# Attention layers of a graph network: windows of nodes divided, turned and counted into the batch statistics while edge rows are still being gathered

## The chip, the cores and the metric

The kernel runs on one core of a Trainium2 chip. The metric is the device time of one execution in microseconds. The engines are TensorE (PE in the profile; PEld is its weight load), VectorE (DVE), ScalarE (ACT), GpSimd (POOL) and SyncE (SP). SBUF and PSUM are the on-chip memories; PSUM has eight banks, B0 to B7 in the code.

## What is computed

A graph with 6250 nodes of 128 features and 100000 edges goes through two relational layers and then, after a layer norm, through two graph attention layers. The change concerns only the attention layers. One of them is, cut to what matters (the edges here include one loop per node):

```python
xw = (x @ W).reshape(n, H, FH)                     # H = 4 heads of 32
al_s = einsum('nhf,hf->nh', xw, a_src); al_d = einsum('nhf,hf->nh', xw, a_dst)
e = leaky_relu(al_s[src] + al_d[dst], 0.2)
m = segment_max(e, dst); ee = exp(e - m[dst]); den = segment_sum(ee, dst)
out = segment_sum((ee / den[dst])[:, :, None] * xw[src], dst) + b
h = elu(batch_norm(out))                           # mean and variance over all nodes
```

The batch norm needs the mean and variance of every feature over all 6250 nodes, so nothing of it can be finished before the last node's sum is.

## The kernel before, in words

The nodes are split into 49 windows of 128 (`NW`). The edges are sorted by destination and cut into 832 slots of 128 edges (`NS`), each of which belongs to one window; 32 slots are a chunk (`CH`), 26 chunks a layer (`NC`). For each slot POOL issues one indirect DMA that gathers 128 rows of 132 numbers into a ring of 96 slots (`Gr`, line 1889); before it reuses a place it waits for the product of the slot 96 earlier, and for the gather 16 earlier.

Per chunk the attention weights of its edges are computed by a chain of small steps in `prep`, which exists once per engine and is run one chunk ahead, a step after each slot. DVE makes the selection matrices (line 937, four per slot in the first eight slots) and the scans of the running maximum (954 to 1006), ACT casts and copies (1368 to 1421), PE transposes (1705, 1726, 1744) and picks the destination's part (1719). DVE then multiplies eight slots' rows at a time by their weights (`weigh`, line 1013).

Per slot, PE multiplies the selection matrix by the gathered rows (line 1770) into bank `s % 3`, and DVE adds the bank into the window's row of the accumulator `AC` (`add`, line 1033), two slots behind (`LAG`). The accumulator holds per window 128 sums, 4 denominators and 4 maxima; the address comes from registers that are loaded 16 at a time. Before PE writes a bank it waits for the addition three slots back. Each engine runs its own list of instructions in the order written here; semaphores are the only coupling.

When all slots are added (end of `gat_vector`'s loop) the end of a layer runs: DVE computes from denominators, maxima and the node's own logits two weights per node and head (lines 1063 to 1082, with an exponential on ACT, line 1430), then POOL multiplies the node's own row by one (line 1904), DVE or POOL the sums by the other (lines 1091, 1906), DVE adds the two (line 1095), PE transposes the windows (line 1781), ACT adds the bias on the way from PSUM to `OT` (line 1435), DVE takes the statistics of four windows at a time (`bn_stats`, line 1098) and aggregates them (line 1101). Then come centring (line 1114), elu, and the projection for the next layer or the output (lines 1120 to 1133).

A list of turns, made on the chip from the sorted edges, says which windows are complete after which slot: `NTURN` is 84 turns for the 49 windows, turn `k` at slot 96 + 9k; a turn without a new window names a spare window. The relational layers already use it. `rest` is a loop over windows that the list left out, skipped by a branch when none was.

## Time and profile before

| what | us |
|---|---|
| median of three timed runs | 5546.97 (5546.96 to 5551.64) |
| the profiled execution | 5593.81 |
| its span, first to last instruction | 5592.0 |
| layer 0 of the attention: first gather to centring | 2764 to 4153 |
| layer 1: first gather to the end | 4181 to 5592 |

Times in views are microseconds from the span's start. "Idle before" is time in which the engine had nothing running, with what ended it; "issue" means that nothing the profile shows ended it, "remote" that the release came from something it cannot name. A wait for several semaphores is put down to the last.

### The profile page before, as it was taken

Reading aid. Unit: us, or ns where it says so; the run is one execution under the profiler, and the core shown is the slowest. Engines: PE = TensorE matmul, PEld = TensorE weight load, DVE = VectorE, ACT = ScalarE, POOL = GpSimd, SP = SyncE. Lnnn points to the kernel's source line nnn. Section 1 sums busy time; section 2 is a strip of 40 time slices with the busy share of each in tenths; the row PEclk is TensorE's granted clock in tenths of the full one; section 3 lists DMA queues with packets and bytes.
Section 4 is the critical chain, followed back from the end, with each engine's and each line's share of the span. In section 5 each row is a group of like instructions: output and inputs, shape, how many; then the busy total and the mean of one; then the engine's idle time right before and its main releaser. Section 6 shows DMA issues by size and latency. Waiting matters only on the chain.

```text
span 5592.0 us, 63654 instructions
## 1 busy us (share of the span) xinstructions
PE 3147.6 (56%) x12887; PEld 2272.1 (41%) x12887; DVE 2561.5 (46%) x9589; ACT 1064.3 (19%) x2505; POOL 3194.9 (57%) x3310
## 2 busy tenths in 40 slices
PE   7946666676734444444415555655651555555555
PEld 3434333343423333333314444444540444444444
DVE  6433333333333443444515555555571555555557
ACT  3301111121200000000102222222230222222223
POOL 0166666666266666666466666666526666666651
PEclk9957777777855555555555555555565555555556
DMA  6513333333322222222122222222102222222221
GB/s 238 228 44 111 124 121 118 118 119 123 115 71 53 55 54 54 55 54 56 35 48 45 45 45 45 45 45 45 39 26 49 46 44 45 45 45 45 45 43 47
DMA packets 168746, 395.78 MB, mean 71 GB/s; under 512 B 57590, under 2 KB 92468, under 8 KB 151092
## 3 DMA queue, kind: packets, MB, share of 16 engines
q0 software_dynamic: 103872, 215.70, 16.8%
q10 hardware_dynamic: 37968, 103.60, 4.8%
q1 hardware_dynamic: 26532, 72.39, 3.5%
q8 instruction: 126, 2.06, 0.2%
q14 instruction: 248, 2.03, 0.1%
HBM read 230.11 MB, written 161.35 MB: 70 GB/s over the span
## 4 chain that ended last, share of the span: by engine, by line
PE 34%; issue 22%; another core or an unknown queue 21%; DVE 13%; ACT 3%; POOL 2%; DVEq 2%; DMA 1%; SPq 1%; ACTq 0%; POOLq 0%
PE B L1770 9%; PE B L1650 8%; PE B L1550 6%; DVE AC L1033 3%; PE B L1612 3%; DVE AC L852 3%; PE B L1705 2%; PE B L1719 2%; ACT hold L1376 1%; POOL Gr L1889 1%; DVE Sr L937 1%; DVEq L308 1%; POOL Gr L1872 1%; DVE Sr L840 1%
## 5 line engine op out<-in xcount | busy, mean ns | idle before, releaser
L1889 POOL DMA_INDIRECT Gr<-Gtab,SRC x1664 | 1617.4, 972 | 1010.6 <-issue 471.4
L1872 POOL DMA_INDIRECT Gr<-Ttab,GID x1568 | 1501.8, 958 | 1045.6 <-issue 413.4
L1650 PE MATMUL B<-Gr,Sr 128*128 x3328 | 916.8, 402 | 723.7 <-issue 381.3
L1770 PE MATMUL B<-Gr,Sr 128*128 128x136 f32 x3328 | 1059.8, 462 | 402.2 <-DVE AC L1033 187.8
L1650 PEld LDWEIGHTS B<-Gr,Sr 128*128 128x128 f32 x3328 | 742.0, 279 | 1104.2 <-issue 1100.0
L1033 DVE TENSOR_TENSOR AC<-AC,B 128x136 f32 x1664 | 486.9, 293 | 1135.1 <-PE B L1770 470.8
L1770 PEld LDWEIGHTS B<-Gr,Sr 128*128 128x128 f32 x3328 | 786.4, 304 | 520.5 <-issue 243.6
L852 DVE TENSOR_TENSOR AC<-AC,B 128x128 f32 x1664 | 476.3, 286 | 937.8 <-remote 400.2
L1550 PE MATMUL B<-XW,hT 128*128 128x512 f32 x672 | 474.5, 798 | 90.3 <-ACT Sr L1202 32.9
L1705 PE MATMUL B<-identb,hold 128*128 128x128 bf16 x1664 | 251.9, 305 | 464.3 <-ACT hold L1376 259.5
L840 DVE TENSOR_SCALAR Sr<-iota,DL 128x128 f32<-128x128 f32 x1664 | 494.3, 299 | 15.8 <-issue 10.9
L1368 ACT CAST hold<-Sr 128x512 bf16<-128x512 f32 x416 | 257.6, 619 | 977.3 <-remote 500.1
L1705 PEld LDWEIGHTS B<-identb,hold 128*128 128x128 bf16 x1664 | 181.3, 138 | 524.5 <-ACT hold L1376 279.5
L937 DVE TENSOR_SCALAR Sr<-iota,DL 128x128 f32<-128x128 f32 x1664 | 373.8, 300 | 19.3 <-issue 18.9
L1202 ACT COPY Sr<-B 128x512 f32<-128x512 f32 x336 | 195.0, 585 | 648.2 <-PE B L1550 396.9
L1376 ACT COPY hold<-B 128x512 bf16<-128x512 bf16 x416 | 240.3, 584 | 147.7 <-PE B L1719 80.1
L1013 DVE TENSOR_TENSOR Gr<-Gr,B 128x1024 f32<-128x1024 f32 x202 | 245.2, 1214 | 3.4 <-issue 3.4
L1719 PE MATMUL B<-A,hold 128*128 x1664 | 163.2, 186 | 97.3 <-issue 44.4
L1719 PEld LDWEIGHTS B<-A,hold 128*128 128x128 bf16 x1664 | 148.1, 119 | 146.7 <-issue 131.7
L524 DVE COPY hT<-B 128x128 f32<-128x128 f32 x217 | 62.5, 289 | 309.2 <-remote 157.7
L1550 PEld LDWEIGHTS B<-XW,hT 128*128 128x128 f32 x672 | 136.8, 252 | 114.6 <-issue 41.7
L1612 PE MATMUL B<-XW,hT 128*128 128x512 f32 x392 | 179.0, 600 | 6.4 <-DVE hT L524 6.4
(275 smaller groups left out, 2358.2 us busy)
## 6 DMA issues: line engine op xcount, KB each, us to landing
Ttab<-Sr ACTq DMA_DIRECT2D x84, 1024.0 KB
Ttab<-Sr SPq DMA_DIRECT2D x51, 1024.0 KB
Gr<-Gtab,SRC POOLq DMA_INDIRECT x1664
Gr<-Ttab,GID POOLq DMA_INDIRECT x1568
Gtab<-Gr ACTq DMA_DIRECT2D x84, 66.0 KB
X1D<-Gr ACTq DMA_DIRECT2D x84, 64.0 KB
Gtab<-XW SPq DMA_DIRECT2D x7, 462.0 KB, 3.7
out<-Sr SPq DMA_DIRECT2D x12, 256.0 KB
```

Of the source, the lines that this page charges most:

```text
L840: e.tensor_scalar(out=selr(sn), in0=iota[:, :], scalar1=DL[:, sn:sn + 1], scalar2=None, op0=ALU.is_equal).then_inc(built_v, 1)
L852: e.tensor_tensor(a, a, B[RGCN_BANKS[L][sa % len(RGCN_BANKS[L])]][:, 0:P], ALU.add).then_inc(slot_add, 1)
L937: e.tensor_scalar(out=sel(s), in0=iota[:, :], scalar1=DL[:, s:s + 1], scalar2=None, op0=ALU.is_equal).then_inc(sel_made, 1)
L1033: e.tensor_tensor(a, a, B[s % 3][:, 0:CW], ALU.add).then_inc(gat_add, 1)
L1550: e.matmul(B[bk][:, :], hT[:, u % 2, :], wl[1][:, i * 512:(i + 1) * 512], start=True, stop=True).then_inc(row_mm, 1)
L1612: e.matmul(B[k][:, :], hT[:, w % 2, :], wl[0][:, k * 512:(k + 1) * 512], start=True, stop=True).then_inc(row_mm, 1)
L1650: e.matmul(B[banks[s % len(banks)]][:, 0:P], selr(s), Gr[:, bass.ds(o, P)], start=True, stop=True).then_inc(slot_mm, 1)
L1705: mm = e.transpose(bt[:, j * P:(j + 1) * P], sbf[:, g % 2, j * P:(j + 1) * P], identb[:, :])
L1719: mm = e.matmul(B[5][:, 12 * m:12 * m + 12], sts[:, g % 2, j * P:(j + 1) * P], A3[:, bass.ds(off(e, regs[m % 16], 12 * NW), 12)], start=Tr ...
L1770: e.matmul(B[s % 3][:, 0:CW], sel(s), Gr[:, (s % GR) * CW:(s % GR + 1) * CW], start=True, stop=True).then_inc(gat_mm, 1)
L1872: e.indirect_dma_start(out=Gr[:, (sn + 1) % TG * P:((sn + 1) % TG + 1) * P], out_offset=None, in_=Tt[L][:, :], in_offset=bass.IndirectOffs ...
L1889: e.indirect_dma_start(out=Gr[:, (s % GR) * CW:(s % GR) * CW + 132], out_offset=None, in_=T2[L][0:NPAD][:, :], in_offset=bass.IndirectOffs ...
```

## The change

Once a group of windows is complete, their weights are computed and the windows are multiplied, turned, biased and counted between the slots, by the list of turns. The table `CLOSE` gives four groups: from slot 400 on the weights for turns 0 to 33, one step per slot, then one turn every four slots from slot 414; turns 34 to 56 from slot 621, 57 to 70 every three slots from slot 741, 71 to 76 from slot 802. Turns 77 to 83 remain for the end, with a fifth round of weights. Every round computes the weights of all 49 windows.

- DVE: `mix` multiplies the window's sums and its own row by their weights into two small buffers; `close` takes the window's statistics two turns later, into the window's own row of `AC`.
- PE: `turn_window` turns both parts with two products against the identity that add up in one bank (2, at the end also 3), so no addition of the parts is left to DVE.
- ACT: `turned_rows` adds the bias and writes the turned window back into `AC`; ACT's steps of `prep` now stand one per slot like the others', with these in between.
- Slot products use banks 0 and 1 instead of 0, 1 and 2, and PE waits for the addition two slots back.
- POOL's multiplications at the end are gone; centring reads `AC` instead of `OT`; the aggregate reads 49 statistics instead of 13; SP issues the loads of `X1D` after the last slot product.

```diff
+CLOSE = ((399, 0, 34, 4), (606, 34, 57, 4), (726, 57, 71, 3), (787, 71, 77, 3))
+WEIGHTS = {b + 1 + i: (j, i) for j, (b, _, _, _) in enumerate(CLOSE) for i in range(14)}
+MIXED = {b + 15 + pace * (k - k0): k for b, k0, k1, pace in CLOSE for k in range(k0, k1)}
+CLOSED = {b + 15 + pace * (k - k0 + 2): k for b, k0, k1, pace in CLOSE for k in range(k0, k1)}
...
+        def weighed(e, j, w):
...
+            return (e.tensor_tensor(heads(part[0][:, j, :]), heads(AC[:, bass.ds(w * CW, P)]), weight(1), ALU.mult),
+                    e.tensor_tensor(heads(part[1][:, j, :]), heads(XW[:, bass.ds(w * CW, P)]), weight(0), ALU.mult))
+
+        def turn_parts(e, j, to):
+            e.matmul(to, part[0][:, j, :], ident[:, :], start=True, stop=False)
+            return e.matmul(to, part[1][:, j, :], ident[:, :], start=False, stop=True)
...
-                e.tensor_tensor(a, a, B[s % 3][:, 0:CW], ALU.add).then_inc(gat_add, 1)
+                if done[1]:
+                    e.wait_ge(endv.sem, done[1])
+                    done[1] = 0
+                e.tensor_tensor(a, a, B[s % 2][:, 0:CW], ALU.add).then_inc(gat_add, 1)
...
+            def mix(k, j):
+                n = L * NTURN + k
+                if k % 8 == 0:
+                    e.reg_load(turns[k // 8 % 2], WIN[0:1, k:k + 8])
+                e.wait_ge(endv.sem, endv.at("al", L * NB + j))
+                if n >= 2:
+                    e.wait_ge(ot_made, n - 1)
...
+                for ins in weighed(e, n % 2, off(e, turns[k // 8 % 2][k % 8], NW + 2)):
+                    ins.then_inc(o_sum, 1)
+
+            def close(k):
+                e.wait_ge(ot_made, L * NTURN + k + 1)
...
+                e.bn_stats(AC[:, bass.ds(w * CW + P, 6)], AC[:, bass.ds(w * CW, P)]).then_inc(bst_made, 1)
...
+                    if s in WEIGHTS:
...
+                        next(closing, None)
+                    if s in CLOSED:
+                        close(CLOSED[s])
+                    if s in MIXED:
+                        mix(MIXED[s], group[MIXED[s]])
...
+            finish(weights(NB - 1))
+            for k in range(LASTK, NTURN + 2):
+                if k >= LASTK + 2:
+                    close(k - 2)
+                if k < NTURN:
+                    mix(k, NB - 1)
+            rest(e, rest3_vector, f"r3v{L}")
...
+            def turn_window(k):
+                n = L * NTURN + k
+                e.wait_ge(o_sum, 2 * n + 2)
+                if n:
+                    e.wait_ge(ot_made, n - 1 if k > LASTK else n)
+                turn_parts(e, n % 2, turning_of(k)).then_inc(o_turned, 1)
...
-                    if s >= 3:
-                        e.wait_ge(gat_add, L * NS + s - 2)
-                    e.matmul(B[s % 3][:, 0:CW], sel(s), Gr[:, (s % GR) * CW:(s % GR + 1) * CW], start=True, stop=True).then_inc(gat_mm, 1)
+                    if s >= 2:
+                        e.wait_ge(gat_add, L * NS + s - 1)
+                    e.matmul(B[s % 2][:, 0:CW], sel(s), Gr[:, (s % GR) * CW:(s % GR + 1) * CW], start=True, stop=True).then_inc(gat_mm, 1)
                     if i < 12 or (i >= 14 and i % 2 == 0):
                         next(gen, None)
+                    if s - 2 in MIXED:
+                        turn_window(MIXED[s - 2])
```

On DVE, in the middle of a chunk of the attention, the list before reads (`L1033` is a slot addition and `L308` the wait and address ahead of it, `L943` a step of `prep`):

```order
L308 ISA [waits gat_added,gat_products]
L1033 TENSOR_TENSOR AC<-AC,B2 128x136
L308 ISA [waits gat_added,gat_products]
L1033 TENSOR_TENSOR AC<-AC,B0 128x136
L943 TENSOR_REDUCE hold<-B5 128x128 [waits prep_vector,prep_tensor]
L308 ISA [waits gat_added,gat_products]
L1033 TENSOR_TENSOR AC<-AC,B1 128x136
```

and in the changed kernel, at a slot that has a turn:

```order
L319 ISA [waits gat_added,gat_products]
L1096 TENSOR_TENSOR AC<-AC,B0 128x136
L1000 TENSOR_REDUCE hold<-B5 128x128 [waits prep_vector,prep_tensor]
L319 ISA [waits end_transposed]
L1167 REGISTER_ALU
L1167 BN_STATS AC<-AC 128x6
L319 ISA [waits bn_stats,end_transposed,end_vector]
L562 ISA
L562 TENSOR_TENSOR hn<-AC,GID 128x128
L563 ISA
L563 TENSOR_TENSOR hT<-XW,GID 128x128
L319 ISA [waits gat_added,gat_products]
```

Three operations, with their waits and address arithmetic, now stand between two slot additions. On PE, at a chunk's end (`L1770` is a slot product, `L1705` a transposition of `prep`), before:

```order
L1770 MATMUL B0<-Gr,Sr 128x136 [waits gat_added]
L1770 MATMUL B1<-Gr,Sr 128x136 [waits gat_added]
L1770 MATMUL B2<-Gr,Sr 128x136 [waits gat_added,weighed_vector]
L1770 MATMUL B0<-Gr,Sr 128x136 [waits gat_added]
L1770 MATMUL B1<-Gr,Sr 128x136 [waits gat_added]
L1705 MATMUL B3<-identb,hold 128x128 [waits prep_scalar]
```

and in the changed kernel:

```order
L1906 MATMUL B1<-Gr,Sr 128x136 [waits gat_added]
L1906 MATMUL B0<-Gr,Sr 128x136 [waits gat_added,weighed_vector]
L566 MATMUL B2<-ident,hn 128x128 [waits end_weighed]
L567 MATMUL B2<-ident,hT 128x128
L1906 MATMUL B1<-Gr,Sr 128x136 [waits gat_added]
L1906 MATMUL B0<-Gr,Sr 128x136 [waits gat_added]
L1834 MATMUL B3<-identb,hold 128x128 [waits prep_scalar]
```

The slot products alternate between two banks, and the turn's two products stand between them.

## Rows read from the trace of the kernel before

**Rows 1.** The page's head and part 1.
```profile
span 5592.0 us, 63654 instructions
PE 3147.6 (56%) x12887; PEld 2272.1 (41%) x12887; DVE 2561.5 (46%) x9589; ACT 1064.3 (19%) x2505; POOL 3194.9 (57%) x3310
```

**Rows 2.** Busy time by stretch: us, engines' busy us (instructions), PEclk, DMA share, GB/s.
```profile
3100.00:3900.00 800.00, 466.57 (x2348) 375.08 (x2348) 413.54 (x1524) 189.38 (x460) 506.33 (x525) 0.54 0.21 45
4062.00:4092.00 30.00, 24.32 (x133) 20.97 (x133) 22.26 (x83) 10.51 (x27) 4.69 (x3) 0.56 0.01 2
4111.40:4153.20 41.80, 13.29 (x49) 8.94 (x49) 39.13 (x53) 10.93 (x17) 22.26 (x16) 0.51 0.00 0
4153.20:4178.00 24.80, 16.03 (x98) 14.02 (x98) 21.33 (x56) 21.11 (x52) 0.00 (x0) 0.84 0.45 128
```

**Rows 3.** The same view of line 1033 (slot additions) alone.
```profile
3100.00:3900.00 800.00, 151.54 (x518) 0.54 0.21 45
4062.00:4092.00 30.00, 8.80 (x30) 0.56 0.01 2
```

**Rows 4.** Waits from 3100 to 3900: us, times, longest.
```profile
DVE AC L1033 <- PE B L1770: 161.0, 114, 7.0
POOL Gr L1889 <- issue: 133.1, 404, 1.6
DVE AC L1033 <- remote: 123.0, 49, 9.6
POOL Gr L1889 <- PE B L1770: 92.5, 86, 5.6
DVE AC L1033 <- DVE AC L1033: 26.1, 109, 0.9
```

**Rows 5.** Line 1387 (first copy of gathered rows): what it waited for, us, times.
```profile
  DMA Gr<-Gtab,SRC: 61.5, 2
```

**Rows 6.** Timeline of DVE, end of layer 0's attention: start, us, instruction.
```profile
4111.44 0.36 DVE L1063 TENSOR_TENSOR Gr<-XW 128x196 f32<-128x196 f32 x1
...
4115.06 0.36 DVE L1076 TENSOR_TENSOR Gr<-AC,Gr 128x196 f32<-128x196 f32 x1 [0.59 <-ACT Gr L1430]
...
4117.86 0.69 DVE L1091 TENSOR_TENSOR AC<-AC,Gr 128x512 f32<-128x512 f32 x1
...
4144.42 7.38 DVE L1098 BATCH_NORM_STATS2 bst<-Gr 128x6 f32<-128x512 f32 x13
4151.84 0.51 DVE L1101 BATCH_NORM_AGGREGATE bmv<-bst 128x2 f32<-128x78 f32 x1
...
4153.20 1.00 DVE L1114 TENSOR_SCALAR Gr<-Gr,bmv,bsc 128x512 f32<-128x512 f32 x2
```

**Rows 7.** Timeline of DVE, two products of one kind in a row.
```profile
4026.03 0.29 DVE L1026 TENSOR_TENSOR AC<-AC,scs 128x128 f32 x1
4026.24 0.16 DVE L1028 TENSOR_TENSOR AC<-AC,scs 128x4 f32 x1
```

**Rows 8.** Timeline of PE, slot products without a pause.
```profile
4019.68 3.59 PE L1770 MATMUL B<-Gr,Sr 128*128 128x136 f32 x14
```

**Rows 9.** Timeline, one slot product and its addition.
```profile
3309.24 0.53 PEld L1770 LDWEIGHTS B<-Gr,Sr 128*128 128x128 f32 x2
...
3309.29 0.80 PE L1770 MATMUL B<-Gr,Sr 128*128 128x136 f32 x2
...
3310.23 0.30 DVE L1033 TENSOR_TENSOR AC<-AC,B 128x136 f32 x1 [0.56 <-PE B L1770]
```

**Rows 10.** Groups: busy us, mean ns (ACT and aggregates).
```profile
L1435 ACT ACTIVATE Gr<-B,gcol 128x128 f32<-128x128 f32 x1 | 0.4, 359 | 0.0
...
L714 DVE BATCH_NORM_AGGREGATE mv<-st 128x2 f32<-128x6 f32 x84 | 15.3, 182 | 2.9
```

**Rows 11.** Timeline of DVE, slot additions back to back.
```profile
4096.15 0.29 DVE L1033 TENSOR_TENSOR AC<-AC,B 128x136 f32 x1 [0.21 <-DVE AC L1033]
```

**Rows 12.** Line 700 (load of eight registers).
```profile
L700 DVEq TENSOR_LOAD <-FF x11: 595/656/742, 1696.3 to 2738.9; - x11
```

More of the change, by code:

```diff
@@ L218, in build @@
         rl = Gr[:, NPAD:NPAD + 2048].rearrange("p (i j e) -> p i j e", i=2, j=2)
-        fin = Gr[:, NPAD + 2048:NPAD + 2048 + 6 * NW * 4].rearrange("p (k e) -> p k e", k=3)
+        fin = GID[:, 0:4 * NW * 4].bitcast(f32).rearrange("p (k e) -> p k e", k=2)
+        largest = wt[:, :, :].rearrange("p a b -> p (a b)")[:, 0:NW * 4].rearrange("p (w h) -> p w h", h=4)
+        share = st6[:, :, :].rearrange("p w k -> p (w k)")[:, 0:NW * 4].rearrange("p (w h) -> p w h", h=4)
+        turning = [B[2 + j][:, 0:P] for j in range(2)]
+        part = [hn[:, :, :], hT[:, :, :]]
+        wci = wc[:, :, :].rearrange("p a b -> p (a b)").bitcast(i32)
+        WIN, RSTW = wci[0:1, 0:NKP], wci[0:1, NKP:NKP + NW]
         flat = [Gr[0:RF, k * RL:(k + 1) * RL] for k in range(9)]
@@ L640, in tables_vector @@
             after("pwk1")
+            then(e.tensor_copy(WIN, PWK), "win")
+            after("win")
+            then(e.scalar_tensor_tensor(out=WIN[:, 1::2], in0=PWK[:, 1::2], scalar=float(NW + 1), in1=PWK[:, 1::2], op0=ALU.is_ge, op1=ALU.add), "win1")
             then(e.tensor_scalar(out=ORD, in0=PWK, scalar1=float(CW), scalar2=None, op0=ALU.mult), "ord")
@@ L893, in vector, with gat_vector @@
             for L in range(2):
-                gat_vector(e, L, vregs)
-        def gat_vector(e, L, vregs):
+                gat_vector(e, L, vregs, (wregs, xregs))
+        def gat_vector(e, L, vregs, turns):
             T = L * NC
@@ new lines, in weights, with ev, past @@
+            def weights(j):
+                def ev(ins, name):
+                    endv.done(ins, name, L * NB + j)
+                    if name in ("z1", "neg", "dn"):
+                        done[1] = endv.at(name, L * NB + j)
+                def past(name):
+                    e.wait_ge(endv.sem, endv.at(name, L * NB + j))
+                if L or j:
+                    e.wait_ge(bst_made, L * (NTURN + 1) + (CLOSE[j - 1][2] if j else 0))
+                ev(e.tensor_tensor(F(0)[:, 0], als, ald_, ALU.add), "z0")
+                yield
+                e.wait_ge(gat_add, L * NS + done[0])
+                ev(e.tensor_tensor(F(0)[:, 1], mmx, ald_, ALU.add), "z1")
+                yield
+                past("z1")
+                ev(e.scalar_tensor_tensor(out=fin[:, 1, :], in0=fin[:, 0, :], scalar=0.2, in1=fin[:, 0, :], op0=ALU.mult, op1=ALU.max), "lr")
+                yield
+                past("lr")
+                e.wait_ge(gat_add, L * NS + done[0])
+                ev(e.tensor_scalar(out=F(0)[:, 0], in0=den, scalar1=0.0, scalar2=-BIG, op0=ALU.is_le, op1=ALU.mult), "neg")
+                yield
+                past("neg")
+                ev(e.tensor_tensor(F(1)[:, 1], F(1)[:, 1], F(0)[:, 0], ALU.add), "pm")
+                yield
+                past("pm")
+                ev(e.tensor_tensor(largest, F(1)[:, 0], F(1)[:, 1], ALU.max), "mx")
+                yield
+                past("mx")
+                ev(e.tensor_tensor(F(0), F(1), largest.unsqueeze(1).to_broadcast([P, 2, NW, 4]), ALU.subtract), "sub")
+                yield
+                yield
+                yield
+                e.wait_ge(end_exp, L * NB + j + 1)
+                e.wait_ge(gat_add, L * NS + done[0])
+                ev(e.tensor_tensor(largest, den, F(1)[:, 1], ALU.mult), "dn")
+                yield
+                past("dn")
+                ev(e.tensor_tensor(largest, largest, F(1)[:, 0], ALU.add), "dn1")
+                yield
+                past("dn1")
+                ev(e.reciprocal(share, largest), "rec")
+                yield
+                past("rec")
+                e.wait_ge(o_sum, 2 * (L * NTURN + (CLOSE[j - 1][2] if j else 0)))
+                ev(e.tensor_tensor(F(0), F(1), share.unsqueeze(1).to_broadcast([P, 2, NW, 4]), ALU.mult), "al")
+                yield
+                yield
@@ L1035, in gat_vector @@
+            def close(k):
+                e.wait_ge(ot_made, L * NTURN + k + 1)
+                w = off(e, turns[k // 8 % 2][k % 8], NW + 2)
+                e.bn_stats(AC[:, bass.ds(w * CW + P, 6)], AC[:, bass.ds(w * CW, P)]).then_inc(bst_made, 1)
+            done = [0, 0]
+            group = {k: j for j, (_, k0, k1, _) in enumerate(CLOSE) for k in range(k0, k1)}
             finish(prep(0))
```

174 lines of the change are left out of this document (90 added, 84 removed).

## The prediction

> **What bounds the kernel now.** First the page's sums: span 5592.0 us, and no engine is full; PE is busy 56% and POOL 57% [rows 1]. The profiled execution took 5593.8 us, the median of the three timed runs is 5547.0, so 47 us less; what I add or take away I put on both alike.
>
> The change touches only the attention, so I next took the busy time by stretch [rows 2]: the steady part of layer 0's gathers (3100 to 3900), a piece in which gathers are no longer issued, and the stretch between the last slot and the centring. In the steady part PE is busy 58%, DVE 52%, POOL 63%: nothing full, so waits decide. The counts of slot additions (line 1033) give the pace [rows 3]: 518 in 800 us, 1.54 us per slot or 49 us per chunk of 32 slots; once gathers have stopped, 30 in 30 us, 1.0 per slot.
>
> Who holds whom? A gather takes POOL 506.33/525 = 0.96 us, plus 0.33 to issue, 1.29 in all, under 1.54; POOL waits 92.5 us for products of PE, that is for a free place among the 96 rows of the ring [rows 2, 4]. The other side does not wait for gathers: the copy that first touches a chunk's gathered rows waited for a DMA only twice, 61.5 us together, once at each layer's start [rows 5]. So **the consumer sets the pace**, PE, DVE and ACT in turn, and not POOL. DVE waits 161.0 us for PE, 123.0 for a release the profile can't name, and 109 of its 518 additions wait only for the addition before them [rows 4]. Every microsecond put into this loop counts unless it falls into one of those waits.
>
> After the last slot comes the piece that the change attacks: the weights from 4111.44, division and sum from 4117.86, statistics from 4144.42, the aggregate at 4151.84, centring at 4153.20 [rows 6]. That is 41.8 us per layer in which PE does 13.29 us of work [rows 2].
>
> **The change, term by term, for one layer (there are two alike).**
>
> *End of the layer, saved.* Left over are one round of weights, 6.4 us (4111.44 to 4117.86, with its 0.59 for the exponential) [rows 6], and 7 of the 84 turns. A turn: two DVE products at 0.21 start to start, taken from two operations of the same kind behind each other [rows 7]; then PE. The slot product runs in two passes, 14 passes in 3.59 us, 0.26 each [rows 8]; the turn is two such products, so four passes, 1.03 us of PE, and 0.85 + 0.51 = 1.36 us from its weight load to its end, by the 0.85 of one two-pass product [rows 9]; then 0.36 on ACT [rows 10], with 0.14 for each handing over (3310.09 to 3310.23) [rows 9]. One turn alone takes 0.42 + 1.36 + 0.36 + 3 x 0.14 = 2.5 us; with two pairs of buffers the next follow at 1.25. Seven: 2.5 + 6 x 1.25 = 10. The aggregate grows from 78 to 294 numbers: 182 ns for 6 and 507 for 78 give 4.5 ns each, so 1.5 us [rows 6, 10]; behind it stay 0.85, and two last statistics and the skipped rest loop are about 1.2 (an estimate: twice 0.28 as of the products, and a register load of 0.66 [rows 12]). Sum 6.4 + 10 + 1.5 + 0.85 + 1.2 = 20, **saved 22**. Bounds: turns at DVE's own 0.63 save 26, turns one after the other at 2.5 save 14.
>
> *77 turns within the slots, added.* On DVE two products and one statistics at 0.21 each, 0.63; on PE 1.03; on ACT 0.36, which at 189.38 busy of 800 has room [rows 2]. The two need not add up, since a turn's stages are slots apart. What covers them: an addition that waits only for its predecessor leaves 0.21 idle [rows 11], and 163 of 518 additions wait for something longer [rows 4]. Without any cover the path takes DVE's 0.63 where DVE leads, PE's 1.03 where PE leads, with full cover nothing. I take 0.5, nearest to DVE's row: PE waits for DVE's additions in order, so a piece put between two additions holds both engines, while PE's own piece can run beside DVE's scans and selections; and a fifth of the additions have their 0.21 to give. 77 x 0.5 = **+38**; bounds 0 and 77 x 1.03 = 79.
>
> *Four more rounds of weights, one step per slot.* Each 6.4 less the 0.59 wait, 5.8 us of DVE [rows 6]; three quarters of it reach the path by the same cover: 4 x 5.8 x 0.75 = **+17**; bounds 0 and 23.
>
> *Register loads.* Eight registers at a time, 0.66 us on DVE's queue, 0.08 per register [rows 12]; ten of these in the loop, about 0.4 each uncovered: **+4**; bounds 0 and 7. The Trainium skill ("Runtime: NRT & Kernel Launch", Instruction fetch mechanics) gives such a load about 200 ns per register, which would be 1.6 us a time and 16 us in place of 7 at most. The trace does not agree, and the row decides.
>
> *Two banks for slot products instead of three.* PE's product of slot s now waits for the addition of s-2, before for s-3. One bank's round is 0.85 from weight load to end, 0.14 to DVE, 0.30 of addition [rows 9]: 1.29 us. By three that is 0.43 per slot, below the 0.50 at which DVE adds back to back (0.29 and 0.21) [rows 11], by two it is 0.645. So each slot that now goes at DVE's 0.50 loses 0.145. These are 109 of 518 at least, 175 per layer, 25 us; all 832 would be 121 us. DVE also holds long pieces (the weighing of eight slots, the scans) behind which PE has two products ready where it had three. I take **+36**, nearer to the counted rows; bounds 0 and 60, since slots with more work than 0.645 in them cannot lose it.
>
> Nothing else is on the path: the last multiplications leave POOL, the loads of X1D on SP are issued earlier, and windows 50 and 51 are cleared at the program's start.
>
> **Sum:** 38 + 17 + 4 + 36 - 22 = 73 to 74 per layer, **148 for both**. The profiled time goes from 5594 to 5742, the median from 5547 to **5695**.
>
> **Rivals.**
> 1. *The two banks cost nothing.* Either the slower slots catch up in the waits for ACT, or PE's clock is granted more: 0.54 in the steady part, so mostly the lower of its two levels (1.2 GHz), 0.84 in the stretch of the elu and the projection [rows 2]; at the higher level a bank's round would be short enough. For it: PE waits for ACT and others, too. Against: rounds above are from the steady part itself. Then 2 x (59 - 22) = +74: 5621.
> 2. *The turning disappears in the waits*, the other side. DVE is idle 48% of the steady part, PE 42% [rows 2]; if each turn falls where its engine waits anyway, only the shorter end is left. It decides from the point where the loop gains less than 22 us per layer, 0.29 us per turn with all else free. Full cover gives 5547 - 44 = 5503. Against: once gathers stop, the same loop is busy 81% and 74% on PE and DVE, so much of the idle time is not in long waits.
> 3. *PE leads.* A turn costs its 1.03 on PE, weights and loads all of their own, banks the upper 60, the end saves 18: 79 + 23 + 7 + 60 - 18 = 151 per layer: 5849. For it: PE is the busiest once gathers stop, and semaphores come late in the steady part (the 123.0 us without a name [rows 4]), against which a third bank was a reserve.
> 4. *The turns are not done early*, so that nothing is saved: the table fixes their slots whatever the data are, so this is out unless a wait holds DVE at the first of a group; it would show as one long gap, and I give it no chance of its own.
>
> **How the numbers follow.** Forecast 0.47, its own range 5640 to 5780 by the bounds of the turn's price (0.3 to 0.65) and of the banks (20 to 50). Rival 1: 0.20. Rival 2: 0.13. Rival 3: 0.20. The range leaves out most of rival 2 and the far part of rival 3: 5550 to 5825. A measurement of this kernel can tell 0.2% (11 us) from no change. Of rival 2, 0.02 end within that, and the bottom of rival 1 adds 0.02, so faster 0.11, same 0.04, slower 0.85.
>
> **What would show it.** Right: the stretch from the last addition to the centring falls to about 20 us; the pace of the slots between 414 and 823 rises by a sixth of a microsecond or more, and that of slots before 400, where only the banks differ, by some 0.04; POOL waits longer for PE. Additions that follow each other stand 0.6 apart, no longer 0.50. Rival 1: slots before 400 keep their pace. Rival 2: all keep it. Rival 3: PE's idle time before slot products is gone. Wrong altogether: a pace set by gathers, with DVE or ACT waiting for DMAs in mid-layer.

## The result and the profile after

| | before | after | ratio, 95% interval |
|---|---|---|---|
| median of the timed runs, us | 5546.97 | 5589.35 | 1.0072 (1.006 to 1.0085) |
| profiled execution, us | 5593.81 | 5595.45 | |

The changed kernel is slower by 42 us (33 to 47 by the interval). The sign was forecast, the size was not: 148 us were expected, 5695 in place of 5589, though the range (5550 to 5825) holds it. The two profiled spans are almost equal by chance: the changed kernel's first slot addition of the attention came 27 us earlier, at 2819.8, while in the other runs with a kernel before at 5547 to 5607 us it comes at 2846 to 2858, with the change and without. So I compare by stretches of the attention.

The page of the kernel after, against [rows 1]: PE has 185 us more to do, DVE 95.
```profile
span 5593.2 us, 66830 instructions
PE 3332.4 (60%) x13461; PEld 2391.0 (43%) x13461; DVE 2656.0 (47%) x10114; ACT 1103.6 (20%) x2656; POOL 3156.6 (56%) x3279
```

Busy time by stretch (columns as in [rows 2]): the steady part, a piece after the last gather with six turns in it, the last slots with the start of the end, and then line 1096, the slot additions, in the first two.
```profile
3100.00:3870.00 770.00, 510.46 (x2391) 400.48 (x2390) 438.50 (x1627) 189.54 (x477) 485.54 (x502) 0.53 0.21 45
4038.00:4068.00 30.00, 22.96 (x133) 19.48 (x134) 20.24 (x80) 11.51 (x26) 0.00 (x0) 0.67 0.00 1
...
4111.50:4130.00 18.50, 9.29 (x38) 6.51 (x36) 11.57 (x34) 1.63 (x4) 0.00 (x0) 0.68 0.00 0
...
3100.00:3870.00 770.00, 146.12 (x500) 0.53 0.21 45
4038.00:4068.00 30.00, 5.79 (x21) 0.67 0.00 1
```
500 slots in 770 us are 1.54 per slot, as before [rows 3], although 41 turns and two rounds of weights lie in them. After the last gather it is 21 slots in 30 us where it was 30.

The waits in 3100 to 3870, a stretch 30 us shorter than that of [rows 4]:
```profile
DVE AC L1096 <- PE B L1906: 146.1, 158, 4.8
...
ACT hold L1478 <- remote: 115.7, 17, 11.0
PEld B L1906 <- DVE AC L1096: 109.4, 114, 5.0
POOL Gr L2023 <- PE B L1906: 95.7, 107, 2.7
...
DVE AC L1096 <- remote: 81.1, 31, 6.2
```
DVE's waits for PE and for releases without a name fell from 161.0 and 123.0 us in 800 [rows 4] to 146.1 and 81.1 in 770, at the same pace: the new work took the place of waits. POOL's wait for PE hardly grew (92.5 to 95.7).

Timeline of DVE at the end of layer 0's attention, to be read against [rows 6]:
```profile
4114.91 0.29 DVE L1096 TENSOR_TENSOR AC<-AC,B 128x136 f32 x1 [0.21 <-PE B L1906]
4115.41 0.29 DVE L1096 TENSOR_TENSOR AC<-AC,B 128x136 f32 x1 [0.21 <-PE B L1906]
...
4118.15 0.35 DVE L1112 TENSOR_TENSOR GID<-XW 128x196 f32<-128x196 f32 x1
...
4124.81 0.29 DVE L562 TENSOR_TENSOR hn<-AC,GID 128x128 f32 x1 [0.27 <-DVE GID L1147]
...
4138.06 0.27 DVE L1208 BATCH_NORM_STATS2 AC<-AC 128x6 f32<-128x106 f32 x1 [0.28 <-DVE AC L1167]
4138.36 1.48 DVE L1211 BATCH_NORM_AGGREGATE bmv<-AC 128x2 f32<-128x294 f32 x1
...
4140.70 1.00 DVE L1224 TENSOR_SCALAR Gr<-AC,bmv,bsc 128x512 f32<-128x512 f32 x2
```
From 4118.15 to 4140.70 are 22.6 us where there were 41.8.

The next table is worked out from the starts of the slot additions (line 1033, then 1096). It gives the microseconds from the addition of one slot to that of another, layer 0 and layer 1. Slots 96 to 400 have only the two banks and ACT's new order of steps as a change; 400 to 741 the first two groups of turns with the gathers running, and three rounds of weights, since the third group's round (slots 727 to 740) stands ahead of its turns; 741 to 831 the last 20 turns and one round. POOL issues its last gather about when slot 737 is added.

| slots | before | after | difference, mean |
|---|---|---|---|
| 0 to 96 | 203.2, 202.5 | 203.1, 204.7 | +1.0 |
| 96 to 400 | 470.2, 468.0 | 465.1, 463.3 | -4.9 |
| 400 to 741 | 514.4, 516.4 | 526.6, 525.5 | +10.7 |
| 741 to 831 | 76.8, 75.6 | 103.4, 102.7 | +26.9 |
| layer 0's last addition to layer 1's first | 149.6 | 130.0 | -19.6 |
| last addition to the end | 68.9 | 48.9 | -20.0 |

So the loop pays +34 per layer and the end gives back 20: 14 per layer, 28 in these two profiled executions, where the timed runs say 42. Most of the price lies in the last 90 slots; 57 turns, three rounds of weights and 741 slots with two banks cost about 7 us together.

### The profile page after: what moved, and what is told of

Same layout as the page of the kernel before. It is cut to its first block, busy times and chain, and to the rows that moved or that the text cites. A ratio compares the mean times of both kernels' runs of the same rounds, so it can differ in the third digit from the quotient of the medians.

```text
span 5593.2 us, 66830 instructions
## 1 busy us (share of the span) xinstructions
PE 3332.4 (60%) x13461; PEld 2391.0 (43%) x13461; DVE 2656.0 (47%) x10114; ACT 1103.6 (20%) x2656; POOL 3156.6 (56%) x3279
## 3 DMA queue, kind: packets, MB, share of 16 engines
q0 software_dynamic: 103872, 215.70, 16.7%
## 4 chain that ended last, share of the span: by engine, by line
PE 39%; issue 20%; another core or an unknown queue 17%; DVE 14%; ACT 3%; DVEq 3%; POOL 2%; DMA 2%; SPq 0%; ACTq 0%; POOLq 0%
PE B L1906 10%; PE B L1779 9%; PE B L1679 6%; PE B L1741 3%; DVE AC L909 3%; DVE AC L1096 3%; PE B L1834 2%; DVE Sr L994 2%; PE B L1848 2%; POOL Gr L2023 2%; DVEq L319 1%; DVE Sr L897 1%; PE B L1657 1%; ACT hold L1486 1%
## 5 line engine op out<-in xcount | busy, mean ns | idle before, releaser
L1906 PE MATMUL B<-Gr,Sr 128*128 128x136 f32 x3328 | 1167.2, 471 | 681.9 <-DVE AC L1096 368.4
L1698 PE MATMUL B<-wx,hT 128*128 128x136 f32 x168 | 67.4, 505 | 188.3 <-DVE hT L576 91.0
```

Of the source, the lines that this page charges most:

```text
L1906: e.matmul(B[s % 2][:, 0:CW], sel(s), Gr[:, (s % GR) * CW:(s % GR + 1) * CW], start=True, stop=True).then_inc(gat_mm, 1)
```

## Experiments

Two theories. **C**, the prediction's (called W in two of the expectations): the consumer (PE, DVE, ACT) sets the pace of the slots, and what is added to it counts unless it falls into a wait. **G**: while gathers run they set the pace, by their bytes, their number or POOL's issue, and only the 90 slots after the last gather are the consumer's. Each group of runs has its own time of the kernel before, taken beside it: 5607 us for the first four runs, 5595 for the next four, 4647, 4647 and 4646 for the last three groups. Ratios are to that time.

### Two banks alone

The kernel before with this alone:
```diff
-                    if s >= 3:
-                        e.wait_ge(gat_add, L * NS + s - 2)
-                    e.matmul(B[s % 3][:, 0:CW], ...
+                    if s >= 2:
+                        e.wait_ge(gat_add, L * NS + s - 1)
+                    e.matmul(B[s % 2][:, 0:CW], ...
```


> The kernel before with two banks for the slot products and nothing else. By the prediction's own term it is 2 x 36 = 72 us slower (5619). If the waits of the loop take that up (or if the loop is paced by the gathers), it is within 0.2% of the kernel before, 5547 +- 11. In the changed kernel the slots 96 to 400, where only the banks differ, kept their pace (465 against 470 us), so I now expect under 12 us.

Measured: 1.0031 (1.0019 to 1.0043), +17 us, 8.7 per layer where the sum had 36. Slots 741 to 831 took 84.4 and 84.3 against 76.8 and 75.6, so 8 us, or 0.09 per slot, nearly all in the stretch without gathers; slots 96 to 400 took 471.7 and 468.8, no difference.

Where slot additions follow each other with nothing between, the price of the bank can be read directly. First b_2banks, the stretch with its granted clock and three of its additions; then the changed kernel in the stretch of the additions shown above:
```profile
4123.80:4131.00 7.20, 6.96 (x22) 5.09 (x21) 3.25 (x11) 0.00 (x0) 0.00 (x0) 0.50 0.00 0
...
4129.21 0.29 DVE L1033 TENSOR_TENSOR AC<-AC,B 128x136 f32 x1 [0.51 <-PE B L1770]
4129.72 0.29 DVE L1033 TENSOR_TENSOR AC<-AC,B 128x136 f32 x1 [0.21 <-PE B L1770]
4130.52 0.30 DVE L1033 TENSOR_TENSOR AC<-AC,B 128x136 f32 x1 [0.51 <-PE B L1770]
```
```profile
4113.80:4118.00 4.20, 3.90 (x16) 2.34 (x16) 2.43 (x9) 0.00 (x0) 0.00 (x0) 1.00 0.00 0
```
At the lower level of PE's clock (0.50) two banks give 0.51 and 0.80 in turn, 1.31 for two slots. That is close to the prediction's 0.645 per slot, where three banks have 0.50 [rows 11]. At the higher level (1.00) additions with two banks stand 0.51 apart, as with three. Over all places in layer 0 where five additions stand in a row, the medians per slot are 0.66 with two banks at the lower level and 0.51 with three (worked out from their starts).

### Half the rows per gather

From slot 96 on each gather fetches 64 rows instead of 128, in the kernel before (b_half) and in the changed one (a_half); the products use old rows for the other half, so other edges are summed.
```diff
-    out=Gr[:, (s % GR) * CW:(s % GR) * CW + 132], ...
+    out=Gr[0:64 if s >= GR else P, (s % GR) * CW:(s % GR) * CW + 132], ...
```


> The kernel before, in which each attention gather from slot 96 on fetches 64 rows instead of 128 (the other half of each slot is left out, the result is not the reference's). If the gathers and what they bring with them set the pace of the slots while they run (theory G), slots 96 to 700 go from 1.54 us to 1.2 or less and the time falls by 200 us or more per layer, over 350 in all. If DVE and PE set it by their own work and their hand-overs (theory W), the pace stays within 5% of 1.54.

> The changed kernel with the same halved gathers. Theory G: with the gathers' delays gone the turning has no cover, the difference to the halved kernel before grows from 42 us to 90 or more. Theory W, waits between PE, DVE and ACT being the cover: the difference stays near 42 us.

Measured: 1.0015 (1.0005 to 1.0024) and 1.0110 (1.0094 to 1.0125); the pair stands 54 us apart, nearer to the 42 of the full pair than to the 90 or more of theory G by bytes. Busy time by stretch of b_half, then its line 1033, then the group of gathers in the same stretch:
```profile
3100.00:3900.00 800.00, 465.25 (x2328) 374.08 (x2328) 419.90 (x1545) 186.06 (x455) 483.54 (x525) 0.54 0.13 23
...
3100.00:3900.00 800.00, 153.32 (x525) 0.54 0.13 23
...
L1889 POOL DMA_INDIRECT Gr<-Gtab,SRC x525 | 483.5, 921 | 316.7 <-issue 147.6 <-remote 109.4 <-PE B L1770 59.7
```
The DMA moves 23 GB/s instead of 45 [rows 2] and the pace is 1.52, nearly as it was. Bytes don't set the pace. The gathers' queue counts 103872 packets as in the kernel before, so the number of packets is not tested by this. An issue of 64 rows still takes POOL 0.92 us, against 0.97.

### Half as many gathers

From slot 96 on every odd slot's gather is left out; its product and addition are made with old rows.
```diff
+                    if s >= GR and s % 2:
+                        continue
                     e.indirect_dma_start(
```


> The kernel before, in which from slot 96 of each layer on every odd slot's gather is left out (736 instead of 1472 gathers from there); its product and its addition are made with whatever rows lie in the ring, so the sums are those of other edges. What PE, DVE and ACT do is unchanged. Theory G (number of gathers): POOL's issue of one gather per slot, with the semaphore updates that come late while gathers run, sets the pace; then the pace of slots 96 to 400 falls from 1.54 toward the 1.0 per slot that stands where no gathers run (1.0 to 1.25), 2 x 736 x 0.3 to 0.5 is 440 to 740 us less than the kernel before. Theory C (the consumer, as in the prediction): the pace stays at 1.5 to 1.55 and the time within 30 us of the kernel before.

> The changed kernel with the same edit: every odd slot's gather from slot 96 on left out, the rest as it was; the sums are those of other edges. Compared with the kernel before under the same edit. Theory G: with the gathers out of the way nothing covers the turning and the lost bank, so this pair differs by much more than the 42 us of the full pair, by 90 to 150 us, as the prediction's terms would have it. Theory C: the difference stays at 40 to 55 us.

Measured: 0.8651 (0.8622 to 0.8679) and 0.9083 (0.9058 to 0.9108). The kernel before lost 754 us, at the upper end of what theory G expected (440 to 740), and the pair lies 242 us apart instead of 42, far more than the 90 to 150 expected. Of b_skip, slot additions and all engines by stretch, the group of gathers, and the longest waits of a_skip (3100 to 3400):
```profile
3100.00:3400.00 300.00, 87.09 (x299) 0.62 0.16 35
...
3100.00:3400.00 300.00, 237.41 (x1321) 200.28 (x1320) 231.97 (x877) 105.90 (x257) 144.84 (x150) 0.62 0.16 35
...
L1894 POOL DMA_INDIRECT Gr<-Gtab,SRC x150 | 144.8, 966 | 155.2 <-PE B L1773 126.9 <-issue 28.3
```
```profile
POOL Gr L2028 <- PE B L1909: 145.2, 91, 4.2
...
DVE AC L1099 <- PE B L1909: 58.6, 103, 2.2
PEld B L1909 <- DVE AC L1099: 50.5, 85, 1.4
```
299 slots in 300 us, with PE busy 79% and DVE 77%: this is the consumer's own pace, and it is the 1.0 of [rows 3] after the last gather. POOL has no releases without a name left to wait for; all its long waits are for PE. **Theory C falls for the kernel before, G stands**, by the number of gathers or what goes with it (the packets fall too, to 80320). And the pair shows what the change costs where nothing covers it, per layer:

| slots | b_skip | a_skip | difference, mean |
|---|---|---|---|
| 96 to 400 | 305.9, 307.0 | 332.7, 331.9 | +25.9 |
| 400 to 741 | 345.1, 343.5 | 421.7, 424.0 | +78.6 |
| 741 to 831 | 74.3, 75.0 | 103.4, 104.4 | +29.3 |

### One half of a turn at a time

The kernel before with two banks, and at the 77 slots of a layer either PE's two products or DVE's three operations of a turn, with results that nobody reads.
```diff
+                    if s - 2 in TURNS:
+                        e.matmul(B[2][:, 0:P], hn[:, 0, :], ident[:, :], start=True, stop=False)
+                        e.matmul(B[2][:, 0:P], hT[:, 0, :], ident[:, :], start=False, stop=True)
...
+                    if s in TURNS:
+                        n = TURNS.index(s)
+                        e.tensor_tensor(hn[:, n % 2, :], XW[...], ones[:, :], ALU.mult)
+                        e.tensor_tensor(hT[:, n % 2, :], XW[...], ones[:, :], ALU.mult)
+                        e.bn_stats(st6[:, n % 2, :], XW[...])
```


> The kernel before with two banks for slot products, and at the 77 slots of a layer at which the changed kernel turns a window PE makes the two products of a turn (of whatever the buffers hold, into a third bank that nobody reads); no DVE or ACT work of a turn, no weights, the end of a layer as before. The two banks alone came to 1.003 of the kernel before. If a turn's PE part is what the slots pay, the 57 early turns cost little (0 to 0.2 each) and the 20 late ones about 0.5 to 1.0 each: 1.003 plus 2 x (6 + 15) = 42 us, 1.009 to 1.011. If DVE's part is what they pay, this kernel stays at 1.003 to 1.005.

> The kernel before with two banks, and at the same 77 slots of a layer DVE makes the two multiplications and the one statistics of a turn into buffers that nobody reads; no PE or ACT work of a turn, no weights, no register loads, the end as before. If DVE's part is what the slots pay: 0.63 us for each of the 20 late turns and 0.1 to 0.2 for the 57 early ones, 2 x (13 + 9) = 44 us over the two banks alone, 1.009 to 1.012. If PE's part is, it stays at 1.003 to 1.005. If both come out at about 1.006, neither leads and the price lies in the holding of both engines.

Measured: 1.0073 (1.0048 to 1.0097) and 1.0067 (1.0043 to 1.0092), so the case "neither leads": either adds some 0.004 to the 1.0031 of the banks, little more than the intervals. In the last 90 slots PE's part takes them from 84.4 and 84.3 to 85.2 and 85.3, DVE's to 88.5 and 86.9, the whole change to 103.4 and 102.7. Of the 19 us between two banks alone and the whole change 14 are in neither part by itself. One round of weights is among them, and it is dearer there than at the end: two of its multiplications run beside three of POOL's.
```profile
4083.53 6.09 POOL L2031 TENSOR_TENSOR Gr<-Gr 128x1024 f32<-128x1024 f32 x3 [75.16 <-ACT scs L1531]
...
4083.80 2.06 DVE L1131 TENSOR_TENSOR GID<-GID,wt 128x392 f32<-128x392 f32 x1
4088.30 1.53 DVE L1140 TENSOR_TENSOR wt<-wt,GID 128x196 f32<-128x196 f32 x1
```
At the end of the layer the same two take 0.57 and 0.36, and the round 5.6 of DVE where it takes 8.2 here, in both layers; the same 8.2 stand in a_half, a_skip and a_again. In a_new, whose last round lies earlier, no such multiplication is slow. The other 6 us may be the handing over from DVE to PE to ACT and back; that was not taken apart further.

### Twenty turns fewer in the loop

The changed kernel with the first two groups only:
```diff
-CLOSE = ((399, 0, 34, 4), (606, 34, 57, 4), (726, 57, 71, 3), (787, 71, 77, 3))
+CLOSE = ((399, 0, 34, 4), (606, 34, 57, 4))
```


> The changed kernel with the first two groups only: 57 turns within the slots, all while gathers are issued, 27 at the end. The trace of the changed kernel puts 27 us per layer on the two late groups (20 turns, two rounds of weights), and at the end a turn costs about 1.25 us: 20 x 1.25 = 25 more there. So within 10 us of the changed kernel (5580 to 5590) if late turns cost the same in both places; 30 us or more slower if a turn at the end costs over 2 us.

Measured: 1.0129 (1.0111 to 1.0147). The end has 27 turns instead of 7 and takes 81.5 us from the last addition, not 48.9: 1.63 per turn, against the 1.25 of the prediction. The last 90 slots fall from 103.4 and 102.7 to 84.7 and 85.1, so 18 us for 20 turns and one round; without the third group's round slots 400 to 741 take 528.9 and 528.1, no less than with it. The two late groups cost 18 us per layer in the loop and save 33 at the end, so they are worth having; what they don't pay for is the lost bank, the early turns and the early rounds.

### POOL's own time, and gathers waited for sooner

A small memset on POOL ahead of every gather, and a wait for the gather 4 or 2 earlier where the kernel before has 16:
```diff
+                        e.memset(mv[:, s % 49, :], 0.0).then_inc(extra, 1)
...
-                    wait_gather(e, n - NSG)
+                    wait_gather(e, n - 4)
```


> The kernel before with one small memset (128x2 numbers that nobody reads) on POOL ahead of every gather from slot 96 of a layer on, 1472 in all. Theory G1 (POOL's own cycle of issue sets the pace): each memset, by some 0.1 to 0.2 us with its dispatch, is added to the pace: 150 to 300 us more. Theory G2 (while POOL issues gathers back to back the other engines' releases come late, and they catch up in POOL's pauses): what fills the time between two gathers replaces a pause, so the time rises by less than the memsets or even falls: -100 to +100 us. Theory C (the consumer sets the pace and POOL has slack): within 15 us of the kernel before.

> The kernel before in which POOL waits, ahead of each attention gather, for the landing of the gather 4 earlier instead of 16 earlier, so that its series of gathers without a pause are broken up. Theory G2: series of 10 to 15 gathers without a pause become short, the stretches in which PE, DVE and ACT all stand still (20% of the steady part) shrink, and the pace falls below 1.54 per slot: 30 to 300 us less. Theory G1: the wait adds to POOL's cycle or does nothing: 0 to 100 us more. Theory C: within 15 us.

> The same with a wait for the gather 2 earlier. If a gather needs over 2.5 us from issue to landing, the pace is set by that: half of it per slot. Theory G2: if the landing takes 2 to 3 us the pace is 1.3 to 1.5 with hardly any stretch in which all engines stand still, and the time is below the kernel before; theory G1: 50 us more or above.

> The changed kernel with the wait for the gather 4 earlier. Theory G2: it gains from the shorter series as the kernel before does, but less, since the turning then has less idle time to fall into: its distance to the kernel before under the same edit grows from 42 us toward the 242 us of the pair with half as many gathers. Theory G1: the distance stays at 42 us.

For this group the kernel before itself took 4647 us, a sixth less than at any time earlier. So these runs could not decide what they were made for, and showed something else. Measured: b_pool 1.0016 (1.0006 to 1.0025), b_fly4 1.0001 (0.9991 to 1.0011), b_fly2 1.0728 (1.071 to 1.0746), a_fly4 0.9984 (0.9974 to 0.9993). b_fly4 equals the kernel before, so its trace stands for that kernel here. First its group of gathers from 2600 to 3200 and the waits there, then b_fly2's group:
```profile
L1889 POOL DMA_INDIRECT Gr<-Gtab,SRC x472 | 456.6, 967 | 144.0 <-issue 92.0 <-PE B L1770 52.0
...
ACT hold L1387 <- DMA Gr<-Gtab,SRC: 132.3, 14, 9.9
...
DVE pen L948 <- ACT hold L1391: 120.2, 14, 9.1
```
```profile
L1889 POOL DMA_INDIRECT Gr<-Gtab,SRC x408 | 391.3, 959 | 209.9 <-DMA Gr<-Gtab,SRC 153.9 <-PE B L1770 44.5 <-issue 11.4
```
POOL now issues one gather after the other, 472 in 600 us, 1.27 each, all 832 of a layer without a pause of 0.5 us, and the copy of a chunk's gathered rows waits for the DMA in every chunk (14 times, 132.3 us), as the prediction's last sentence had it for the case "wrong altogether" (two waits only in the run of [rows 5]). With a wait for two gathers back the pace is 600/408 = 1.47, so from a gather's issue until its landing has released POOL about 2.9 us pass (an estimate: twice the pace). The memsets fill the 0.3 us that POOL is idle between two issues:
```profile
3299.26 0.96 POOL L1895 DMA_INDIRECT Gr<-Gtab,SRC  x1 [0.19 <-PE B L1770]
3300.22 0.11 POOL L1893 MEMSET mv<- 128x2 f32 x1
3300.53 0.96 POOL L1895 DMA_INDIRECT Gr<-Gtab,SRC  x1 [0.19 <-POOL mv L1893]
```
1.27 from issue to issue with the memset as without, which is why 1472 of them cost 7 us.

What is the difference between the two conditions, the long one (the kernel before at 5547 to 5607 us) and the short one (4646 to 4647)? The same lines of the page, of the kernel before (5592), of b_skip and of b_fly4, the chain that ended last by engine:
```profile
PE 34%; issue 22%; another core or an unknown queue 21%; DVE 13%; ACT 3%; POOL 2%; DVEq 2%; DMA 1%; SPq 1%; ACTq 0%; POOLq 0%
```
```profile
PE 38%; issue 19%; DVE 16%; another core or an unknown queue 15%; DVEq 3%; ACT 3%; POOL 3%; DMA 1%; SPq 1%; ACTq 0%; POOLq 0%
```
```profile
PE 38%; issue 18%; DMA 15%; DVE 13%; POOL 9%; ACT 3%; DVEq 3%; SPq 1%; ACTq 0%; POOLq 0%
```
In the kernel before a fifth of the chain is releases that the trace cannot name, and in b_fly4 none; b_skip keeps 15%, most of it (606 us) in the relational layers, which its edit leaves as they were; in its attention these releases are 135 us of the chain, in that of the kernel before 676. A piece of the timeline of the kernel before shows what they look like (POOL, then PE, DVE and ACT):
```profile
3301.63 0.95 POOL L1889 DMA_INDIRECT Gr<-Gtab,SRC  x1 [0.30 <-issue]
3302.89 0.95 POOL L1889 DMA_INDIRECT Gr<-Gtab,SRC  x1 [0.30 <-issue]
3304.15 0.95 POOL L1889 DMA_INDIRECT Gr<-Gtab,SRC  x1 [0.30 <-issue]
3308.03 0.95 POOL L1889 DMA_INDIRECT Gr<-Gtab,SRC  x1 [2.92 <-PE B L1770]
...
3299.47 0.80 PE L1770 MATMUL B<-Gr,Sr 128*128 128x136 f32 x2
...
3299.48 0.87 DVE L937 TENSOR_SCALAR Sr<-iota,DL 128x128 f32<-128x128 f32 x4
3307.39 0.30 DVE L1033 TENSOR_TENSOR AC<-AC,B 128x136 f32 x1 [7.04 <-PE B L1770]
...
3303.82 0.62 ACT L1368 CAST hold<-Sr 128x512 bf16<-128x512 f32 x1 [6.45 <-remote]
```
The product ended at 3300.27 and DVE started the addition that waits for it at 3307.39; ACT stood until 3303.82 for selections of which DVE had made the last by 3300.35. In such gaps PE, DVE and ACT stand still together: from 3100 to 3900 that is 158 of 800 us (20%, worked out from the union of their busy times), in b_skip 2% of 3100 to 3700, after the last gather (4032 to 4111) 5%. With two banks alone it is 134 us, in the changed kernel 101: there the slower slots and the turning went. In the short condition the three stand still together for 18% of 2600 to 3200 too, but there the wait has a name, the DMA above.

### The changed kernel again, and two versions of it

> The changed kernel once more, on the chip of this group. On the chips seen first the kernel before took 5547 to 5607 us and the changed one 42 us more; on the chip of the last group the kernel before took 4647, POOL issued gathers back to back at 1.28 us per slot, and no release came late. Where the kernel before takes about 5600 here, this one is at 1.006 to 1.009 of it. Where it takes about 4650, POOL's issue alone sets the pace of slots 96 to 736, only the last 90 slots and the end count: plus 16 and minus 20 per layer, 0.997 to 1.000.

> The kernel before with the wait for the gather 4 earlier, again. Where the kernel before takes about 5600: theory G2 (the late releases come from long series of gathers without a pause) expects series of at most 4 and 30 to 300 us less; if the late releases have another cause that only goes along with the gathers, the time stays within 30 us. Where it takes about 4650: 1.000 as before.

> The changed kernel with three banks for slot products again; the windows are turned in free columns of the banks of the preparation (B5 and B7), at slots where that bank is not otherwise in use. Theory: the lost bank is worth 8 to 9 us per layer of the changed kernel's time, so 15 to 20 us less than the changed kernel on the same chip; if the turning itself is the whole price, no difference.

> The same with three banks, and other groups: turns 34 to 56 every three slots, turns 57 to 66 from slot 708 on, while gathers still run, 67 to 73 from slot 768, and ten turns left for the end. Ten turns and one round of weights leave the stretch without cover (0.7 to 0.9 us a turn, 5 a round), three more turns stay for the end (1.63 each): 6 to 10 us per layer less than with three banks alone. On a chip with the kernel before at about 5600 it comes to 0.998 to 1.003 of it, on one at 4650 to 0.987 to 0.993.

The three-bank versions turn a window into free columns of B5 or B7, whichever the preparation does not use at that slot, and PE waits there for the last reader of the bank:
```diff
-        turning = [B[2 + j][:, 0:P] for j in range(2)]
+        turning = [B[7][:, 0:P], B[3][:, 0:P], B[5][:, 384:512]]
...
+                if k < LASTK and turning_of(k) is turning[2]:
+                    e.wait_ge(pv.sem, pv.at("ad", T + TURNED[k] // CH + 1))
+                    last_turn[1] = n + 1
+                else:
+                    e.wait_ge(pa.sem, pa.at("sc", ...
+                    last_turn[0] = n + 1
```
and a_new has other groups besides:
```diff
+CLOSE = ((399, 0, 34, 4), (606, 34, 57, 3), (693, 57, 67, 3), (753, 67, 74, 3))
```
In a_new the last round of weights begins at slot 754 in place of 788, and ten turns are left for the end in place of seven.

Measured, with the kernel before at 4647: a_again **0.9981** (0.9972 to 0.999), b_fly4_2 1.0003 (0.9994 to 1.0012), a_3b 0.9966 (0.9954 to 0.9978), a_new **0.9944** (0.9931 to 0.9958). The same change that costs 42 us in the one condition saves 7 to 9 in the other (7 by the medians, 9 by the ratio). By the starts of the additions, per layer:

| slots | b_fly4 | a_again | a_3b | a_new |
|---|---|---|---|---|
| 96 to 400 | 391.5, 389.0 | 391.6, 387.4 | 393.2, 389.7 | 393.4, 389.4 |
| 400 to 741 | 428.5, 425.3 | 434.6, 431.1 | 434.8, 430.9 | 438.6, 435.3 |
| 741 to 831 | 92.6, 92.3 | 106.0, 106.2 | 101.4, 98.6 | 86.9, 87.2 |
| between the layers; end | 133.4; 68.9 | 113.9; 48.8 | 113.9; 48.9 | 118.6; 53.4 |

With POOL's issue in the lead two banks cost nothing in 304 slots, and the first 741 slots pay 6 us for 57 turns and three rounds. In the last 90 slots the price is 14 instead of 27: in this condition the last gather is issued only when slot 782 is added (738 in the long one), so nearly half of them still run at POOL's pace. The third bank gives 8 us in all, half of what was expected; the other groups give 9 more. With ten turns moved ahead of slot 741, three to the end, and the last round moved under the gathers and away from POOL's multiplications, the last 90 slots are 13 us shorter per layer, of which the slots 400 to 741 take back 4 and the three more turns at the end 4.6.

> The regrouped kernel with three banks again, in the hope of a chip on which the kernel before takes about 5600. There: banks about 0, early turns and rounds plus 10 to 12 per layer, seven late turns and a round plus 10, the end minus 15: 5 to 7 us per layer more than before, 1.000 to 1.003. On a chip with about 4650: 0.994 again.

> The kernel before with the wait for the gather 4 earlier. Where the kernel before takes about 5600: if the late releases come from long series of gathers without a pause, 30 to 300 us less; if they have another cause, within 30 us. Where it takes about 4650: 1.000.

Both met the short condition again (the kernel before at 4646): 0.9943 (0.993 to 0.9957) and 1.0003 (0.9994 to 1.0012). So a_new beats both kernels where the gathers run at POOL's pace. Whether it does so with the kernel before at 5600 was not measured.

## Why the prediction was wrong

**The step that failed** is "So the consumer sets the pace, PE, DVE and ACT in turn, and not POOL", with what was drawn from it, "Every microsecond put into this loop counts unless it falls into one of those waits". It put 95 us per layer on the loop (38 + 17 + 4 + 36); 34 were measured. It rested on POOL's 1.29 us per gather being under 1.54, and on a copy that does not wait for gathers. Both are true, and yet half as many gathers take the pace from 1.54 to 1.0. What I took for the consumer's own waits (161.0 for PE, 123.0 without a name, in 800 us [rows 4]) came with the gathers: in b_skip DVE's additions wait 73.4 us for PE in 500, and of the releases without a name 0.5 us is left on all engines. The hint stood in [rows 2, 3]: without gathers a slot took 1.0. I used the busy shares of that stretch against rival 2 and gave no reason for its pace. Per slot PE is busy 0.90 us in the steady part and 0.81 in that stretch, DVE 0.80 and 0.74, so the work was nearly the same, and it was idle time that had gone.

- *The end, saved 22*: right, 20 by both ends (bounds 26 and 14). Within it the weights took 6.7 for 6.4, the aggregate 1.48 for 1.5, and the seven turns with the last statistics 13.6 (4124.81 to 4138.36) for 11.2.
- *77 turns, +38*, and *four rounds, +17*: as prices without cover they were if anything low. By a_skip, slots 400 to 741 lose 78.6; less 341 slots of two banks at 0.085 (29) and three rounds at 4.3 (13) that leaves 37 for 57 turns, 0.64 each where I had 0.5. With gathers running the same turns, rounds and banks cost 10.7 together. The wrong part was how many turns pay in full: about 20 of 77.
- *Two banks, +36*: measured 8.7 (b_2banks). The price at slots that go at DVE's own pace was right, 0.15 at the lower level of the clock, and is nothing at the higher one, as rival 1 had it. Spread over all slots without cover it is 0.085 each (25.9/304 in a_skip, where ACT's order differs too; 0.09 in b_2banks), twice the 0.04 that 36 over 832 slots means, so uncovered it would be 70. With gathers it is nothing. So this term, too, failed by its cover. "Additions that follow each other stand 0.6 apart" holds in b_2banks; the changed kernel's last additions of layer 0 stand 0.51 apart because the granted clock was 1.00 there.
- *Register loads, +4*: not measured apart.
- *Rival 1* (banks cost nothing, 5621) came nearest in its time, within 32 us, but by the reason of rival 2: the turning of 57 windows disappeared in the waits. Its sign, slots before 400 that keep their pace, was seen. *Rival 2* named the mechanism and its point of decision (22 us per layer); the loop gained 34 because the last 90 slots have hardly any such waits. In the condition of 4647 it came true: the loop pays about 20 per layer and the result is below before. *Rival 3* (PE leads) is not shown by any run; that the loop pays over 130 per layer in a_skip lies between the prediction's 95 and this rival's 169 and does not tell which engine leads. That the price depends on the stretch, full after the last gather and nearly none before, was no case of mine; each rival had one price for all slots.
- "POOL waits longer for PE" was right by 3 us only; the rise of "a sixth of a microsecond or more" between slots 414 and 823 holds for the last 90 slots alone (0.3 each).

**Still open**: why releases come late in the one condition. Not the bytes (b_half), and not long series of gathers without a pause as such: in the other condition all 832 of a layer pass with no late release. In the long condition it goes with the number of gathers per slot (b_skip), but the gathers, their packets and POOL's issuing were halved together and are not told apart. The same program ran in both conditions. The record numbers the chips 0 and 7 in the long one and 9, 0 and 3 in the short one, so the number does not tell the condition; that it belongs to the chip, as some expectations assume, is not shown.

## What to carry to other kernels

Before an added instruction is given a price, find the pace of the same loop in a stretch where a suspected resource is at rest, and compare the busy shares: if the same work runs faster there, the idle time elsewhere belongs to that resource and is cover. Then price the added work by where it lands: here slots 400 to 741 paid 11 us for what cost 79 with half the gathers, and behind the last gather the price was full, so work that must be inserted goes ahead of that point. An experiment that halves a suspect's count while the rest stays the same settles in one run what the waits by name do not.

## What the runs showed of the hardware

- One and the same kernel took 5547 to 5607 us on some occasions and 4646 to 4647 on others, with nearly the same busy times: DVE 2561.5 and 2541.1, POOL 3194.9 and 3198.1 us (kernel before, and b_fly4 for the short condition).
- In the long condition releases between engines come late while POOL issues gathers, by 7 us in the piece shown, for PE, DVE and ACT at once; the three stand still together 20% of the time, with half the gathers 2%. In the short condition (18%) they wait for the DMA, and no release comes late.
- An indirect gather costs POOL 0.97 us for 128 rows and 0.92 for 64, and 1.27 from issue to issue; a memset of 0.11 us between two is free. POOL is released by its landing about 2.9 us after its issue (estimate from b_fly2).
- Products into two banks instead of three, each followed by a DVE addition of 0.29 us: 0.66 against 0.51 us per slot at a granted clock of 0.50, 0.51 against 0.51 at 1.00.
- Two DVE multiplications took 2.06 and 1.53 us in place of 0.57 and 0.36 while POOL multiplied 128x1024 numbers three times.
- Turns one after the other at the end cost 1.63 each with two buffers (a_g2), though DVE's share is 0.63; in the trace of the changed kernel DVE waits 0.2 to 1.8 us for ACT ahead of most of their statistics.
